# Expert mixing on one NeuronCore: contracting over 64 rows in two row halves of the TensorE array instead of over 128 rows

## The reference, cut to what matters

```
h = relu(x @ gate_w1.T + gate_b1);  g = (h @ gate_w2.T + gate_b2).mean(axis=1)     # g: [32, 8]
mW1 = W1 + einsum('be,efh->bfh', g, TW1)      # 32 matrices 512x128, TW1: 8 x 512 x 128
mW2 = W2 + einsum('be,ehf->bhf', g, TW2)      # 32 matrices 128x512, TW2: 8 x 128 x 512
u = gelu(x @ mW1.T + mb1);  out = u @ mW2.T + mb2
```

## Time and profile before

| | us |
|---|---|
| two runs | 773.96, 773.03 (median 773.5) |
| span of the profiled execution | 772.4 |
| TensorE busy (matmul passes) | 701.8 |
| VectorE busy | 582.3 |
| mean granted TensorE clock, share of 2.4 GHz | 0.968 |
| attention pipeline, to the first mix | about 588 |
| four groups with their mixing | about 184 |

### The profile page before, as it was taken

One profiled execution on the slowest core, in us unless ns is written; L12 is line 12 of the kernel. 1 busy time (PEld: TensorE's weight loads), 2 busy tenths in 40 slices (PEclk: granted clock), 3 DMA queues, 4 the chain that ended last, 5 costly groups with the idle time before them and its releaser, 6 DMA issues.

```text
span 772.4 us, 21515 instructions
## 1 busy us (share of the span) xinstructions
PE 701.8 (91%) x7542; PEld 505.3 (65%) x7542; DVE 582.3 (75%) x1313; ACT 371.3 (48%) x878; POOL 292.9 (38%) x351
## 2 busy tenths in 40 slices
PE   5239989999999999999999999999977999999998
PEld 3016656655666656666566666566647989898996
DVE  5326879999989999999999899998885537264542
ACT  2015646555665556655566655566541342433133
POOL 4205635544556445555445564455541000000000
PEclk9569999999999999999999999999996999999999
DMA  3764933222222222232222322222250010000101
GB/s 89 206 73 77 122 57 78 52 60 48 48 65 64 54 54 48 54 75 51 58 48 48 72 57 55 54 48 53 65 62 1 1 35 20 27 27 14 28 20 48
DMA packets 85316, 42.79 MB, mean 55 GB/s; under 512 B 40552, under 2 KB 83880, under 8 KB 85168
## 3 DMA queue, kind: packets, MB, share of 16 engines
q1 hardware_dynamic: 83840, 36.21, 20.7%
q0 software_dynamic: 1456, 6.31, 5.2%
HBM read 16.13 MB, written 8.40 MB: 32 GB/s over the span
## 4 chain that ended last, share of the span: by engine, by line
PE 52%; DVE 22%; issue 10%; POOL 8%; DMA 3%; ACT 2%; SPq 1%; DVEq 1%; POOLq 0%; ACTq 0%
DVE mx L561 10%; PE SB L888 8%; PE SB L836 7%; PE WB L824 7%; DVE xn_d L555 5%; PE WB L975 5%; PE SB L932 4%; PE WB L811 4%; PE SB L811 4%; POOL rstd_d L340 2%; PE WB L1006 2%; POOL rstd_a L340 2%; DMA KBD<-KM 2%; PE SB L936 2%; PE SB L1016 2%
## 5 line engine op out<-in xcount | busy, mean ns | idle before, releaser
L888 PE MATMUL SB<-KBD,QT 128*32 128x512 f32 x1024 | 118.2, 603 | 22.6 <-DMA KBD<-KM 21.6
L347 POOL TENSOR_TENSOR KM<-K_ch,bd_scale 128x1024 f32<-128x1024 f32 x32 | 60.6, 1894 | 142.9 <-ACT K_ch L413 142.9
L561 DVE TENSOR_REDUCE mx<-SB 128x8 f32<-128x512 f32 x128 | 86.7, 678 | 22.9 <-PE SB L888 22.9
L888 PEld LDWEIGHTS SB<-KBD,QT 128*32 128x32 f32 x1024 | 30.6, 111 | 106.3 <-issue 106.3
L506 ACT ACTIVATE Pr<-WB,mb1T 128x256 f32<-128x256 f32 x128 | 49.9, 478 | 75.3 <-PE WB L824 75.3
L360 POOL TENSOR_TENSOR PT_sum<-PT 128x512 f32<-128x512 f32 x64 | 82.1, 1302 | 10.3 <-ACT PT L448 10.3
L568 DVE TENSOR_TENSOR Pr<-SB,mx 128x512 f32<-128x512 f32 x128 | 84.1, 677 | 0.0
L405 ACT ACTIVATE Pr<-Pr 128x512 f32<-128x512 f32 x128 | 80.9, 632 | 5.0 <-DVE Pr L568 1.7
L639 DVE RECIPROCAL rden<-SB 128x256 f32<-128x256 f32 x32 | 56.2, 1757 | 18.9 <-PE SB L936 18.9
L448 ACT COPY PT<-SB 128x512 f32<-128x512 f32 x128 | 65.1, 597 | 0.0
L901 PE MATMUL SB<-ident,Pr 128*128 128x128 f32 x512 | 61.8, 273 | 1.4 <-ACT Pr L405 1.4
(11 more groups left out here) (190 smaller groups left out, 1484.0 us busy)
## 6 DMA issues: line engine op xcount, KB each, us to landing
KBD<-KM SPq DMA_DIRECT2D x128, 128.0 KB, 2.4
x_all<-in_L_attn_x SPq DMA_DIRECT2D x32, 128.0 KB, 2.1
v_rows<-V_rows SPq DMA_DIRECT2D x32, 128.0 KB, 1.8
TW<-in_L_ffn_TW POOLq DMA_DIRECT2D x16, 256.0 KB, 8.7
VBD<-v_rows SPq DMA_DIRECT2D x128, 32.0 KB, 1.9
GA<-ga_rows POOLq DMA_DIRECT2D x1, 2048.0 KB, 9.9
out_x<-attT SPq DMA_DIRECT2D x16, 128.0 KB, 1.8
out_x<-y_ga SPq DMA_DIRECT2D x16, 128.0 KB, 1.8
```

Of the source, the lines that this page charges most:

```text
L561: nc.vector.tensor_reduce(mx[:, k, :], SB[k][:].rearrange("p (h j) -> p h j", h=8), AX.X, ALU.max).then_inc(mx_ready, 1)
L888: last = mm(SB[k][W * q:W * q + W, :].rearrange("p (h j) -> p h j", h=8), QT[hh][:, W * blk:W * blk + W], KBD[:, 8 * hh:8 * hh + 8, W * bl ...
```

## The change

The mixing contracts over 64 partitions instead of 128. J becomes 8: partitions 0 to 63 hold 8 experts x 8 rows of one half of the matrix (r = 0), partitions 64 to 127 the same of the other half (r = 1). A matmul of the mixing takes 64 rows of weights (still 128 columns wide) and 64 moving columns (8 j x 8 batch rows). `mix(g, pair)` fills two banks, one from each half, and takes turns between them matmul by matmul: 8 matmuls for a bank, 16 for a pair. `mix_done` still counts banks; both banks of a pair end one matmul apart. For mW1 the even banks are now rows 0 to 255 and the odd ones rows 256 to 511, so `ffn1(g, 0)` waits for other counts. The expert loads become 32 DMAs of half the size (8 partitions instead of 16). TensorE's loop over the first three groups is written out; the other engines keep theirs.

```diff
@@ -31,7 +31,7 @@
-    J = P // E
+    J = HALF // E
...
-        TW1 = sb("TW1", [P, F // J, D])
-        TW2 = sb("TW2", [P, D // J, F])
+        TW1 = sb("TW1", [P, F // (2 * J), D])
+        TW2 = sb("TW2", [P, D // (2 * J), F])
...
-        e_rows = sb("e_rows", [E, E, J])
+        e_rows = sb("e_rows", [E, 2, E, J])
...
             def load_experts(e):
-                pool.dma_start(TW1[J * e:J * e + J], ins["L0_ffn_TW1"][e].rearrange("(i j) h -> j i h", j=J)
-                               ).then_inc(tw_loaded, 16)
-                pool.dma_start(TW2[J * e:J * e + J], ins["L0_ffn_TW2"][e].rearrange("(i j) f -> j i f", j=J)
-                               ).then_inc(tw_loaded, 16)
+                for r in range(2):
+                    rows = slice(HALF * r + J * e, HALF * r + J * e + J)
+                    pool.dma_start(TW1[rows], ins["L0_ffn_TW1"][e].rearrange("(r i j) h -> r j i h", r=2, j=J)[r]
+                                   ).then_inc(tw_loaded, 16)
+                    pool.dma_start(TW2[rows], ins["L0_ffn_TW2"][e].rearrange("(r k j) f -> r j k f", r=2, j=J)[r]
+                                   ).then_inc(tw_loaded, 16)
...
                 if m < 8:
-                    dst = mW1[:, :, m * 64:(m + 1) * 64].rearrange("p b r -> p r b")
-                    base = W1T[:, m * 64:(m + 1) * 64]
+                    row = m % 2 * (F // 2) + m // 2 * 64
+                    dst = mW1[:, :, row:row + 64].rearrange("p b r -> p r b")
+                    base = W1T[:, row:row + 64]
...
-            def mix(g, m):
-
-                for k in range(4):
-                    if m < 8:
-                        lhsT = TW1[:, 4 * m + k, :]
-                    else:
-                        c, half = divmod(m - 8, 2)
-                        lhsT = TW2[:, 4 * half + k, c * P:(c + 1) * P]
-                    last = mm((WB if m < 8 else SB)[m % 4][:, k * P:(k + 1) * P], lhsT,
-                              Gd[:, bass.ds(g * (J * GB), J * GB)], start=True, stop=True)
-                last.then_inc(mix_done, 1)
+            def mix(g, pair):
+
+                cols = slice(g * J * GB, (g + 1) * J * GB)
+                for k in range(HALF // J):
+                    for r in range(2):
+                        rows = slice(HALF * r, HALF * r + HALF)
+                        if pair < 4:
+                            lhsT = TW1[rows, pair * (HALF // J) + k, :]
+                        else:
+                            lhsT = TW2[rows, k, (pair - 4) * P:(pair - 3) * P]
+                        bank = (WB if pair < 4 else SB)[(2 * pair + r) % 4]
+                        last = mm(bank[:, k * J * GB:(k + 1) * J * GB], lhsT, Gd[rows, cols], start=True, stop=True)
+                        if k == HALF // J - 1:
+                            last.then_inc(mix_done, 1)
...
-                        pe.wait_ge(mixed, g * 16 + max(2 * (c + 1), 5 + c // 2))
+                        pe.wait_ge(mixed, g * 16 + (5, 7, 7, 8)[c])
...
-                for m in range(8, 16):
-                    if m >= 12:
-                        pe.wait_ge(mixed, g * 16 + (m - 3))
-                    mix(g, m)
+                for pair in range(4, 8):
+                    if pair >= 6:
+                        pe.wait_ge(mixed, g * 16 + (2 * pair - 2))
+                    mix(g, pair)
...
-            with pe.Fori(0, NG - 1) as g:
-                group(g, False)
-            group(NG - 1, True)
+            for g in range(NG):
+                group(g, g == NG - 1)
```

More of the change, by code:

```diff
@@ L247, in adaln_block @@
         N_G = N_G0 + 1 + (NG - 1) + FC + 1
-        N_MOD, N_ATTN, N_W, N_TW = 16 * len(mod_w), 16 * len(attn_w), 16 * len(rest_w), 16 * 2 * E
+        N_MOD, N_ATTN, N_W, N_TW = 16 * len(mod_w), 16 * len(attn_w), 16 * len(rest_w), 16 * 4 * E
         @block.sync
@@ L751, in after @@
                     beside(nc.vector.tensor_scalar(GKBD[NL:P], bc(tri[NL:P, NL:P], [NL, LH, NL], 1), 1.0, BIG, ALU.subtract, ALU.mult))
-                    beside(nc.vector.tensor_copy(e_rows[:], bc(ident[0:E, 0:E], [E, E, J], 2)))
+                    beside(nc.vector.tensor_copy(e_rows[:], bc(ident[0:E, 0:E], [E, 2, E, J], 1, 3)))
                     then(nc.vector.tensor_reduce(jmask[:], ident[:].rearrange("p (e j) -> p j e", j=J), AX.X, ALU.add))
@@ L1008, in step @@
                 if isinstance(it, int) and it == B + 3:
-                    for m in range(2, 4):
-                        mix(0, m)
+                    mix(0, 1)
                 if has(it, 4):
@@ L1039, in experts @@
                 rows, biases = (WB[2], SB[3]) if g0 == 0 else (SB[1], SB[2])
-                mm(rows[:, 0:n_b], e_rows[:].rearrange("e k j -> e (k j)"), gT[:, cols], start=True, stop=True
+                mm(rows[:, 0:n_b], e_rows[:].rearrange("e r k j -> e (r k j)"), gT[:, cols], start=True, stop=True
                    ).then_inc(g_done, 1)
@@ L1054, in after @@
                     pe.wait_ge(yga_ready, B)
-                    for m in range(2):
-                        mix(0, m)
+                    mix(0, 0)
                 if it == B + 3:
-                    for m in range(4, 8):
-                        pe.wait_ge(mixed, m - 3)
-                        mix(0, m)
+                    for pair in range(2, 4):
+                        pe.wait_ge(mixed, 2 * pair - 2)
+                        mix(0, pair)
                     experts(1, NG, N_G0)
@@ L1098, in group @@
                     if not last and j == GB - 2:
[L1099 to L1103, removed]
+                        for pair in range(2):
+                            pe.wait_ge(gelu_done, g * (FC * GB) + FC * (GB - 1 + pair))
+                            mix(g + 1, pair)
                     if not last and j == GB - 1:
-                        for m in range(4, 8):
-                            pe.wait_ge(mixed, g * 16 + (16 + m - 3))
-                            mix(g + 1, m)
+                        for pair in range(2, 4):
+                            pe.wait_ge(mixed, g * 16 + (16 + 2 * pair - 2))
+                            mix(g + 1, pair)
                     if j >= 1:
```

## The result

The changed kernel took 818.8 us (813.6 and 823.9 in two runs) against 773.5 us: 1.058 times as long, 95% interval 1.054 to 1.062. The forecast was 784 with a range to 803, so it failed on the size: the loss is 45 us, not 10. Timed again in four executions, the same kernel gave a median of 820.4 us (809.8 to 823.4).

What follows compares the result with a forecast made beforehand. TensorE was taken to bound the last quarter, its mixing paced by loading 128 weight columns (111 ns a pass). Terms 1.5 + 2.0 + 4.4 + 2.0 + 0.5 = +10.4 us on a 772.4 us span gave 784 us, range 767 to 803.

Steps and rivals of the forecast that it cites:

- Step (4), the loads: Expert loads: four more POOL issues at each of four load points, same bytes; +0.5 us (0 to +2.8).
- The clock rival: Mixing: half-filled array brings the half clock back in every group, doubling 55 us of mixing; 839 us, chance 3%.
- (1) Passes: Mixing on TensorE: loads of both row halves overlap, each of 512 rounds loses 3 ns; +1.5 us (0 to +5.1).
- (2) Changes of shape: Around the mixing's 13 runs: 26 changes of array shape at 0.09 us each; +2.0 us (0 to +2.5).
- (3) VectorE's pairs: Adds of mixed banks come due in twos, so TensorE waits in mixing, ffn2(0) and ffn1(0); +4.4 and +2.0 us.
- (5) The loop: TensorE's written-out group loop: saved register instructions are hidden under a TensorE that is never idle; 0.
- The serial rival: Mixing: weight loads of the two row halves go one after another, a pair takes 3.57 us; 839 us, chance 13%.

Runs made afterwards that it cites:

- a_loads16_fill: Changed kernel with the earlier 16 loads of 16 partitions and 13 extra matmuls, results unread, in TensorE's idle time before the first mix: 781.8 us, 1.009.
- a_fill: Changed kernel with its own 32 loads of 8 partitions, plus 13 extra matmuls, results unread, in TensorE's idle time before the first mix: 800.4 us, 1.034.
- a_again: The changed kernel itself, unaltered, timed again in four executions: 820.4 us.
- b_loads32_8part: Kernel before, mixing unchanged, with only its expert loads cut into 32 DMAs of 8 partitions: 792.1 us, 1.024.
- g0cols64: Changed kernel with the earlier loads of 16 partitions and group 0 mixed over all 128 rows with 64 moving columns a matmul: 812.4 us, 1.045.

## Why the prediction was wrong

The account, in medians: 773.9, + 7.9 for the halves with the clock held (`a_loads16_fill`), + 18.6 for the loads (`a_fill`), + 20.0 for the clock (`a_again`) = 820.4 us. The 7.9 is 9.8 for four groups less the 2 that the extra matmuls give back; those 2 are then in the 20.0, so against the kernel before the clock costs about 18.

**Step (4), the loads, failed**, and it is the first 18 us. It said that the bytes are the same, allowed up to 2.8 us for the issues and up to 4 us either way for the first KBD transfer. The issues were indeed nothing: in the changed kernel KM follows the last one without idle time, 1.1 us later than before where 0.7 was forecast, and the 16-partition version has as many. The first KBD transfer was no loss either (17.16 us in `b_loads32_8part`). But the sentence on bytes took the rate for granted, and the transfers of `v_rows` and `VBD` beside the later loads, where the 18 us went, had no term. The text even reckoned with loads at half rate for the last point and found 12 us of cover there, and that cover held, but it carried only half of one point's 8 us over to the early pipeline, where three load points have none. The earlier trace rows held the rate, 111 GB/s; the halving of the partitions in the diff was the only other thing needed, with the rule on ports of the Trainium skill, "SBUF — State Buffer", Door 1.

**The clock rival, given 3%, was the other half of the miss**: the sum had no term for the clock, and it cost 10 to 20 us. The rival was priced for every group (55 us) and dismissed because the four-tile stretches ran at 1.00. Those stretches show that tiles do not bring a clock down. The question was whether the new passes would bring it back up from the half clock that the earlier trace rows show at 588 us, and for that the pipeline's rows are no evidence: they start at full clock. It happened in group 0 alone. The rival named the half-filled array as the reason; g0cols64 shows the same low clock with all rows filled.

**(1) Passes:** right. 112.5 ns a round against a forecast 114.6, so + 0.5 us where 1.5 stood. The loads of two row halves do run side by side, and no gain came: the 128-column load is the limit, as line 1043 showed. The up to 2x of the Trainium skill, "TensorEngine Tiling (Array Packing)", Theoretical Speedup, did not show in this trace. The Trainium skill, "TensorEngine Tiling (Array Packing)", Key Properties, says that different tiles load and multiply in parallel; the trace agrees where passes alternate (56 ns), and hardly where they don't (94 ns).

**(2) Changes of shape:** right in kind, too small. Of the 0.82 us a group, the rounds take 128 x 0.9 ns = 0.12; the other 0.70 lie at six changes, 0.12 us each where 0.09 was read. For 26 changes that is an estimate of 3.0 us against 2.0, above the bound of 2.5. That (1) and (2) together come to the forecast 3.5 is luck: one was too high by what the other was too low.

**(3) VectorE's pairs:** right in kind and place. Adds follow at (3.70 - 1.05) / 3 = 0.88 us, as taken; by its starts TensorE is delayed 0.41 us in the mixing (forecast 0.4), 0.76 in `ffn2(0)` (0.85) and 0.41 in `ffn1(0)` (0.45). The table's 1.60 us a group make 6.4 us for four, as forecast (4.4 + 2.0).

**(5) The loop:** right, 0.

With neither of the two misses in it, the changed kernel would take 773.9 + 9.8 = 783.7 us, an estimate from the length of the groups; it measures 781.8 us with the extra matmuls (`a_loads16_fill`), and the forecast was 784. The sum was right for the stage that it looked at, and wrong for what lay outside. The serial rival (839 us, 13%) was wrong as the change stands: most of its mechanism appears when the order of issue is changed (94 ns a pass), and the alternation in `mix` avoids it.

## What to carry to other kernels

When a layout is changed for the sake of one engine, price the transfers that fill it anew, by partitions reached and not by bytes: here 18 of the 45 us came from loads of 8 partitions in place of 16, most of them 450 us and more ahead of the mixing that wanted them. Where a stretch starts at the low clock, ask what brings the clock back and whether the new instructions still do. Splitting the contraction pays nothing while the weight load of the full output width sets the pace, and banks handed over in pairs make the next engine late. When a variant ends with the time of before, look whether a gain hides a loss: the length of one group told here what the medians hid.

## What was not expected of the hardware

- Loads issued by POOL to 8 partitions moved 48 to 67 GB/s with the DMA engines full, to 16 partitions 111 GB/s, for the same bytes in DMAs of the same 128 KB; the packets differ too (2736 and 1712).
- In group 0, with passes of 64 moving columns in the mixing, TensorE was busy 10.00 of 10 us at a granted 0.50 for 40 us and more; with passes of 128 columns in the same place the clock was at 1.00 within 10 us. Where alternating passes of 64 columns began at 1.00 (`a_loads16_fill`, groups 1 to 3 of the changed kernel) it stayed there; with one half after the other it fell to 0.51 (680 to 690 us) under a TensorE busy 10.00 of 10 us.
- Two row halves overlap almost fully when their passes alternate (56.2 ns a pass), and mostly don't when one half's eight passes precede the other's (94 ns).
- A change between 64-row and full-array matmuls cost about 0.12 us (26 of them, an estimate of 3.0 us).
